# Seven block products for the gate and up projections of a dense layer, and another order of the work where the attention begins

## What is computed

```python
Wg = (gate_w.astype(float32) - 128.0) * gate_scale[:, None]   # 2048 x 512, int32 weights
Wu = (up_w.astype(float32) - 128.0) * up_scale[:, None]       # 2048 x 512
Wd = (down_w.astype(float32) - 128.0) * down_scale[:, None]   # 512 x 2048
h = silu(x @ Wg.T) * (x @ Wu.T)
x = layernorm(x + h @ Wd.T)
```

## Time and profile before

| | |
|---|---|
| median of 3 runs | 2914.81 us (2914.24 to 2915.42) |
| the profiled execution | 2915.48 us |
| its span, first to last instruction | 2913.7 us |
| TensorE busy | 2875.1 us, 99% of the span |
| VectorE, ScalarE, GpSimd busy | 2190.2, 1463.0 and 1416.7 us |
| mean granted clock of TensorE | 0.997 |
| dense layer, from the gate and up of unit 2 | 384.4 us to 785.1 us |
| slots of the attention | from 785.1 us |

### The profile page before, as it was taken

One profiled execution on the slowest core, in us unless ns is written; L12 is line 12 of the kernel. 1 busy time (PEld: TensorE's weight loads), 2 busy tenths in 40 slices (PEclk: granted clock), 3 DMA queues, 4 the chain that ended last, 5 costly groups with the idle time before them and its releaser, 6 DMA issues.

```text
span 2913.7 us, 39448 instructions
## 1 busy us (share of the span) xinstructions
PE 2875.1 (99%) x13614; PEld 2383.3 (82%) x13614; DVE 2190.2 (75%) x3048; ACT 1463.0 (50%) x3034; POOL 1416.7 (49%) x971
## 2 busy tenths in 40 slices
PE   9999999999999999999999999999999999999998
PEld 8887888888888888888888888768777887888886
DVE  6899433333589999999999999887657677766665
ACT  6655312121466666666666666655544444544443
POOL 7886322222334444444444444557544555655553
PEclk9999999999999999999999999999999999999999
DMA  3000100000132222222222222221111111211111
GB/s 135 1 22 26 64 22 22 22 22 8 47 99 64 72 62 62 72 64 62 69 66 62 65 79 61 77 80 52 51 51 44 58 51 44 73 65 58 51 51 44
DMA packets 78181, 160.40 MB, mean 55 GB/s; under 512 B 11168, under 2 KB 19744, under 8 KB 76960
## 3 DMA queue, kind: packets, MB, share of 16 engines
q1 hardware_dynamic: 77984, 157.88, 17.9%
HBM read 115.63 MB, written 8.65 MB: 43 GB/s over the span
## 4 chain that ended last, share of the span: by engine, by line
PE 92%; DVE 5%; ACT 1%; issue 1%; DMA 0%; POOL 0%; SPq 0%; POOLq 0%; DVEq 0%; ACTq 0%
PE OP L44 8%; PE OP L45 8%; PE OP L46 8%; PE B L44 5%; PE B L46 5%; PE A L44 5%; PE A L46 5%; PE B L45 5%; PE A L45 5%; PE S L1054 3%; PE S L1056 3%; PE S L1055 3%; PE S L1718 2%; PE S L45 2%; PE S L46 2%; PE S L44 2%
## 5 line engine op out<-in xcount | busy, mean ns | idle before, releaser
L1130 DVE SCALAR_TENSOR_TENSOR x_tok<-OP,expert_weight,x_tok 128x512 f32<-128x512 f32 x252 | 188.3, 748 | 144.8 <-PE OP L46 144.5
L1009 POOL TENSOR_TENSOR middle_w_lo<-second_raw,middle_w_hi 128x512 fp32r<-128x512 f32 (+1 forms) x96 | 144.8, 1510 | 223.2 <-ACT middle_w_hi L1004 223.2
L2465 POOL TENSOR_TENSOR lag_rnorm<-lag_norm,minus_half 128x8 f32<-128x8 f32 x64 | 105.9, 1654 | 302.0 <-DVE lag_norm L2763 302.0
L771 POOL TENSOR_TENSOR ffn_in_lo<-ffn_inner,ffn_in_hi 128x512 fp32r<-128x512 f32 x64 | 85.6, 1338 | 335.9 <-ACT ffn_in_hi L767 335.8
L1102 POOL TENSOR_TENSOR middle_in_lo<-middle_slot,middle_in_hi 128x512 fp32r<-128x512 f32 x128 | 168.0, 1312 | 137.6 <-ACT middle_in_hi L1098 136.6
L44 PE MATMUL B<-xT_hi,lag_w_hi 128*128 128x512 f32 x512 | 206.7, 404 | 1.8 <-DVE lag_c L2528 1.8
L44 PE MATMUL A<-xT_hi,lag_w_hi 128*128 128x512 f32 x512 | 200.9, 392 | 0.0
L46 PE MATMUL B<-xT_hi,lag_w_lo 128*128 128x512 f32 x512 | 200.8, 392 | 0.0
L46 PE MATMUL A<-xT_hi,lag_w_lo 128*128 128x512 f32 x512 | 200.5, 392 | 0.0
L45 PE MATMUL B<-xT_lo,lag_w_hi 128*128 128x512 f32 x512 | 199.5, 390 | 0.0
L45 PE MATMUL A<-xT_lo,lag_w_hi 128*128 128x512 f32 x512 | 199.5, 390 | 0.0
(11 more groups left out here) (550 smaller groups left out, 9020.1 us busy)
## 6 DMA issues: line engine op xcount, KB each, us to landing
lag_raw<-in_head_weights SPq DMA_DIRECT2D x64, 256.0 KB, 4.4
lag_b_row<-lag_b_scratch SPq DMA_DIRECT2D x64, 256.0 KB, 3.2
lag_rot_q<-lag_r SPq DMA_DIRECT2D x128, 128.0 KB, 2.3
lag_rot_k<-lag_r SPq DMA_DIRECT2D x128, 128.0 KB, 2.4
middle_down_raw<-in_expert_down SPq DMA_DIRECT2D x32, 512.0 KB, 3.5
middle_raw<-in_expert_in SPq DMA_DIRECT2D x32, 384.0 KB, 2.9
second_raw<-in_expert_in SPq DMA_DIRECT2D x32, 384.0 KB, 3.0
ffn_raw<-in_dense_gate SPq DMA_DIRECT2D x8, 512.0 KB, 3.5
```

The costliest lines, as they stand in the source:

```text
L1009: pool.tensor_tensor(self.w_lo[q % 2][:, out], self.raw[q % 2][:, of], f32(self.w_hi[q % 2][:, out]), ALU.subtract).then_inc(self.s_wlo, 1)
L1130: dve.scalar_tensor_tensor(row, self.down_bank(v, n), self.expert_weight[:, e:e + 1], row, op0=ALU.mult, op1=ALU.add).then_inc(self.s_acc, 1)
L2465: pool.tensor_tensor(rnorm[f.rbuf], norm2, half[:, 0:2 * TPB], ALU.pow).then_inc(s_rn, 1)
```

## The change

Units 0 and 1 (LEADING = 2, four chunks) stay as they are. The other twelve chunks go through seven block products as in the experts, for two batches at a time: 24 steps q, of which q % 2 is the pair of batches and q // 2 the chunk (`DensePairs`). A step has down products of one chunk, 8 tiles of 3 matmuls, each with an add of its own by VectorE. There is one buffer for the weights and one for their parts; the sums S1 to S3 are written into the place of their own low parts. Since the activations stay the same for all chunks, their four sums for each pair are made once (`DenseRows`), by VectorE, in ten subtractions and additions of 128x1024 for each pair, from the high and low parts, with four high parts by ScalarE and four low parts by VectorE. This lies within the end of unit 0 and unit 1.

TensorE's order at the end: the turn of batch 0 stands between the down tiles of the last step, the turn of batch 1 moves into slot 0 behind the first factor row, the turn of batch 2 behind the second, and batch 3 stays. The norms follow. In unit 0, ScalarE makes the high part of batch 2's second chunk ahead of the norm's rows of batch 3, no longer behind them. The rest of the attention and the experts stay. The diff is cut; the waits of `DenseRows.second`, `third` and `fourth` are of the kind of `first`.

```diff
+    def first(self, dve, p):
+        v = self.value
+        dve.wait_ge(self.turned.s_lo, (2 * p + 2) * TPB)
+        self.step(dve, p, "T1", v("hi", p, "B12"), v("hi", p, "B11"), ALU.subtract)
+        dve.wait_ge(self.s_sum, self.summed(p, 1))
+        self.step(dve, p, "T1", v("lo", p, "T1"), v("lo", p, "B12"), ALU.add)
+        dve.wait_ge(self.s_sum, self.summed(p, 2))
+        self.step(dve, p, "T1", v("lo", p, "T1"), v("lo", p, "B11"), ALU.subtract)
...
+    BLOCK = 2 * P
+    PARTS = {1: ("A11", "B11", 0), 2: ("A12", "B21", 1), 6: ("S2", "T2", 0), 7: ("S3", "T3", 0),
+             5: ("S1", "T1", 2), 4: ("A22", "N4", 0), 3: ("S4", "B22", 2)}
...
+    RAW = ("A21", "A11", "A12", "A22", "S4")
+    GROUPS = ((0, 2), (2, 5), (5, 7))
...
+    def sums(self, dve, w):
+        part, out = self.part, self.summed
+        at = self.mats + 6 * w
+        if w:
+            self.done(dve, 7, 2 * w - 1)
+        else:
+            self.closed(dve)
+        dve.wait_ge(self.s_sum, at + 1)
+        dve.tensor_tensor(out("S1"), part("A21"), part("A22"), ALU.add).then_inc(self.s_sum, 1)
+        dve.tensor_tensor(out("S3"), part("A11"), part("A21"), ALU.subtract).then_inc(self.s_sum, 1)
+        dve.wait_ge(self.s_sum, at + 2)
+        dve.tensor_tensor(out("S2"), out("S1"), part("A11"), ALU.subtract).then_inc(self.s_sum, 1)
+        dve.wait_ge(self.s_sum, at + 4)
+        dve.tensor_tensor(part("S4"), part("A12"), out("S2"), ALU.subtract).then_inc(self.s_sum, 1)
...
+    def split_hi(self, act, w, n):
+        act.wait_ge(self.s_sum, self.mats + 6 * w + (1, 4, 5)[n])
+        if w:
+            self.done(act, (2, 7, 3)[n], 2 * w - 1)
+        else:
+            self.closed(act)
...
+    def split_lo(self, pool, w, n):
+        pool.wait_ge(self.s_whi, self.mats + 4 * w + n + 1)
+        if n == 1:
+            pool.wait_ge(self.s_sum, self.mats + 6 * w + 5)
+        out, of = self.group(n)
+        pool.tensor_tensor(self.w_lo[:, out], of, f32(self.w_hi[:, out]), ALU.subtract).then_inc(self.s_wlo, 1)
...
+        out, first = self.bank(n, q), p in self.OPENS
+        pe.wait_ge(self.s_wlo, self.mats + 4 * (q // 2) + self.NEEDS[p])
+        if q < 2 and x in self.rows.ORDER:
+            pe.wait_ge(self.rows.s_lo, self.rows.place(q, x))
+        if p == 1:
+            pe.wait_ge(self.s_in, self.products + (2 * (q - 2) + 1 if q > 1 else 0))
+        elif p == 2 and q > 1:
+            pe.wait_ge(self.s_c, self.at["c", 11, q - 2])
+        elif p == 5 and q > 1:
+            pe.wait_ge(self.s_c, self.at["c", 12, q - 2])
+        elif p in (2, 5) and q == 1:
+            pe.wait_ge(self.s_acc, self.tiles_before - TPB + n)
+        elif p in (6, 7, 4):
+            pe.wait_ge(self.s_act, self.at["act", {6: "snap1", 7: "snap2", 4: "snap3"}[p], q])
+        elif p == 3:
+            pe.wait_ge(self.s_c, self.at["c", 22, q])
...
+        if self.closes(q):
+            pe.wait_ge(self.s_in, self.products + 2 * self.last)
+            pe.wait_ge(self.s_acc, self.tile(q, n) - 3)
+        else:
+            pe.wait_ge(self.s_acc, self.tile(q, n) - 1)
...
+    def tiles(self, q, p):
+        if q < 1:
+            return ()
+        if q == self.last:
+            return [(q - 1, n) for n in {4: (4, 5), 3: (6, 7)}.get(p, ())]
+        if q == self.last - 1:
+            return ([(q - 1, n) for n in {1: (0, 1), 2: (2, 3), 4: (4, 5), 3: (6, 7)}.get(p, ())]
+                    + [(q, n) for n in {5: (0,), 7: (1, 2, 3)}.get(p, ())])
+        return [(q - 1, n) for n in {1: (0,), 2: (1,), 4: (2,), 3: (3,), 6: (4,), 5: (5,), 7: (6, 7)}[p]]
...
-                sp.wait_ge(dense.s_wlo, (UNITS - 1) * 3)
+                sp.wait_ge(dense.s_deq, LEADING * 3)
+                pairs.load(sp, 0, a["dense_in"])
+                pairs.load_out(sp, 0, a["dense_out"])
+                for w in range(1, DENSE_CHUNKS):
...
+                for q in range(pairs.last):
+                    for p in (1, 2, 4, 3, 6, 5, 7):
+                        pairs.product(pe, p, q if p in (4, 3) else q + 1)
+                        for step, n in pairs.tiles(q, p):
+                            pairs.down(pe, step, n)
+                for p in (4, 3):
+                    pairs.product(pe, p, pairs.last)
+                    for step, n in pairs.tiles(pairs.last, p):
+                        pairs.down(pe, step, n)
+                for first, tiles in ((0, (0,)), (2, (1, 2)), (4, (3,))):
+                    pairs.down(pe, pairs.last, first)
+                    pairs.down(pe, pairs.last, first + 1)
+                    turn1.turn(pe, 0, [A, T, S1, O], norm1.s_row, lambda t: pe.wait_ge(
+                        pairs.s_in, pairs.products + 2 * pairs.total), tiles)
+                pairs.down(pe, pairs.last, 6)
...
-                        pe.wait_ge(turn1.s_lo, max(f.s + 1, 2) * TPB)
+                        pe.wait_ge(turn1.s_lo, (f.s + 1) * TPB)
                     until(pe, s_cv, f.s * TAPS)
                     projection(f, 0, A, s_a1)
                     until(pe, s_sz, f.s - 1)
+                    if f.s == 0:
+                        pairs.added(pe, pairs.last, TPB)
                     if f.s == 1:
                         pe.wait_ge(turn1.s_lo, BATCH * TPB)
                     projection(f, 1, B, s_a2)
                     if f.s == 0:
...
+                        pe.wait_ge(turn1.s_lo, 2 * TPB)
+                        factors.product_row(pe, 1)
+                        turn1.turn(pe, 2, [S0, S1, T, O], norm1.s_row)
                         factors.turn_row(pe, 1)
```

ScalarE in the steps, and its order where slot 0 begins; then VectorE's:

```diff
+                for q in range(pairs.last):
+                    pairs.snap(act, 1, q + 1)
+                    if q % 2:
+                        if q < pairs.last - 1:
+                            pairs.split_hi(act, (q + 1) // 2, 1)
+                    else:
+                        pairs.down_split_hi(act, q // 2)
+                    pairs.silu(act, 0, q + 1)
+                    if q % 2 == 0 and q < pairs.last - 1:
+                        pairs.split_hi(act, (q + 2) // 2, 0)
+                    pairs.high(act, 0, q)
+                    if q == 0:
+                        pairs.snap(act, 2, 1)
+                    pairs.silu(act, 1, q)
+                    if q % 2 and q < pairs.last - 1:
+                        pairs.split_hi(act, (q + 1) // 2, 2)
+                    if q:
+                        pairs.snap(act, 2, q + 1)
+                    pairs.high(act, 1, q)
+                    pairs.snap(act, 3, q + 1)
+                pairs.done(act, 7, pairs.last - 1)
+                split_head(0, 0, range(5))
+                factors.split_hi(act)
+                pairs.high(act, 0, pairs.last)
+                norm1.normalise(act, 0, tiles=(0,))
+                pairs.silu(act, 1, pairs.last)
+                norm1.normalise(act, 0, tiles=(1,))
...
                         norm1.normalise(act, 3, tiles=(0, 1))
-                        factors.row(act, 0)
-                        norm1.normalise(act, 3, tiles=(2, 3))
-                        turn1.high(act, 2)
...
-                        if u == UNITS - 1:
-                            dense.added(dve, u, t)
-                            norm1.statistics(dve, t)
-
+                pairs.dequantise(dve, 0)
+                chunks_of(dense, 1, 1)
+                dense.add(dve, 1, 0)
+                dense_rows.low(dve, 0, "T1")
+                dve.wait_ge(dense.s_u, FPU * (BATCH + 2))
+                dense_rows.fourth(dve, 0)
+                dense_rows.low(dve, 0, "T2")
+                chunks_of(dense, 1, 2)
+                dve.wait_ge(dense.s_wlo, 6)
+                dense_rows.first(dve, 1)
+                dense.add(dve, 1, 1)
+                dense_rows.low(dve, 0, "T3")
+                dense_rows.low(dve, 0, "N4")
+                dense_rows.second(dve, 1)
+                chunks_of(dense, 1, 3)
+                pairs.sums(dve, 0)
+                dense.add(dve, 1, 2)
+                dense_rows.third(dve, 1)
+                dense_rows.low(dve, 1, "T1")
+                pairs.corner(dve, 11, 0)
+                dense_rows.fourth(dve, 1)
+                dense.add(dve, 1, 3)
+                dense_rows.low(dve, 1, "T2")
+                pairs.dequantise_out(dve, 0)
+                dense_rows.low(dve, 1, "T3")
...
+                for q in range(pairs.last):
+                    pairs.corner(dve, 22, q)
+                    if q % 2 == 0:
+                        if q < pairs.last - 1:
+                            pairs.dequantise(dve, (q + 2) // 2)
+                    elif q < pairs.last - 1:
+                        pairs.sums(dve, (q + 1) // 2)
+                    tile_adds(q, 1)
+                    pairs.corner(dve, 11, q + 1)
+                    tile_adds(q, 2)
+                    pairs.inner(dve, 0, q)
+                    tile_adds(q, 4)
+                    pairs.corner(dve, 12, q)
+                    if q == 0:
+                        dense_rows.low(dve, 1, "N4")
+                    tile_adds(q, 3)
```

(51 more changed lines are left out.)

425 lines of the change are left out of this document (340 added, 85 removed).

## The result

The changed kernel takes 2888.80 us in the median of 4 runs (2886.67 to 2889.11), against 2915.11 us (2914.24 to 2916.76) for the kernel before beside it. The ratio is 0.9906, with a 95% interval from 0.9895 to 0.9918: 26.3 us less, where 25.7 were forecast. The profiled execution took 2888.55 us, its span is 2886.8.

The account below looks back on a forecast made before the run. The prediction took TensorE, busy 99% of the span, as the bound: -32.6 + 1.2 + 3.0 + 2.7 = -25.7 us, from 2914.8 to 2889 us. Four cases in five lie between 2882 and 2900.

Parts of the forecast that it names:

- The matmuls: Dense layer: block products remove 144 gate and up matmuls at 0.2267 us each, -32.6 us.
- The steady state: Middle dense steps of 14.96 us: VectorE's 11 to 12.5 us fit and weight swaps have 1.5 to 2.4 slack; nothing lost.
- both rivals that end near or above the time before: Stalls at each of 11 weight swaps, 2922 us, chance 0.05; stalls of about 1 us in all 24 steps, 2913, chance 0.05.
- the second: Stalls of about 1 us in every one of 24 steps from pairs of adds on two banks, 2913 us; chance 0.05.
- Going in: Entry to the new steps: product 3 of step 0 waits for VectorE's corner 22, +1.2 us.
- Ahead of the attention: Last step before the attention: TensorE waits for an add and for the turned rows' low parts, +3.0 us, bounds 0 and 6.
- Slot 0: Attention's first slot: VectorE's statistics delay the taps, and the turn of the squares waits for ScalarE; +2.7 us, bounds 0 and 6.
- No clock lost: Whole kernel: granted clock stays at 1.00, as single waits are 1.4 us at most; nothing added.

Follow-up runs that it names:

- experiment 1: Kernel before, with 144 gate matmuls of units 2 to 7 left out and nothing else changed; 2883.21 us against 2915.81.
- experiment 4: Changed kernel with six extra VectorE operations ahead of the third block sums of the second pair of batches; 2890.46 us.
- experiment 3: Changed kernel with six extra GpSimd operations ahead of its low part of S1 to S3 at each of 11 weight swaps; 2903.18 us.
- experiment 8: Changed kernel with six extra VectorE operations behind corner 22 in each of 23 steps; 2918.85 us, ratio 1.0012.
- 2: Changed kernel with three extra GpSimd operations ahead of its low part of S1 to S3 at each of 11 weight swaps; 2887.63 us.
- 6: Changed kernel with VectorE reordered ahead of the attention: first inner part and an add before batch 0's last two statistics, batch 1's first two later; 2890.70 us.
- 9: Changed kernel with the order ahead of the attention changed on VectorE, GpSimd, ScalarE and TensorE; 2889.89 us.
- 10: Changed kernel with VectorE's statistics of batch 3 behind slot 0's first taps and ScalarE's rows of batch 3 behind both squares; 2887.13 us.
- 12: Changed kernel with three extra VectorE operations behind corner 22 in each of 23 steps; 2889.33 us.
- 5: Changed kernel with VectorE's statistics and aggregates of batch 3 moved from ahead of slot 0's first taps to behind them; 2887.26 us.
- 7: Changed kernel with both VectorE reorderings: ahead of the attention, and batch 3's statistics behind slot 0's first taps; 2891.04 us.

## Why the prediction was right

**The matmuls** (-32.6): right, shown by experiment 1, to 0.1 us in its trace. A step is 14.96 us, there are 13470 matmuls.

**The steady state** (nothing lost): right. VectorE has 10.7 us of 14.96 to do on average, just under the 11 to 12.5 given. The slack at the swap is 2.8 us, more than the 1.5 to 2.4 counted: every sum took its 0.41 us and GpSimd stood still, as had been taken, and ScalarE's high part starts behind S2, the third sum, and not behind the fourth. The mechanisms of both rivals that end near or above the time before exist, and were a measured distance away: 2.8 us at the swap, about 1.8 in an odd step. The prediction gave both 0.05; the second is the nearer.

**Going in** (+1.2): no wait, so this term was wrong in size. VectorE kept to the forecast's times up to the low part of T1 (over at 391.4, as forecast), where block sums below the assumed 1.3 made up for two weight sums of 1.5 us (the 382.22 row is one). What failed lies behind it: `fourth` took 2.4 us in place of 3.6, since no wait for GpSimd came, and two low parts, the dequantising and the corner took 0.5 less than counted, which makes the 1.8 us by which corner 22 was over ahead of 402.0. Product 3, due at 400.9 by the forecast, came at 401.28. The mechanism was right, as experiment 4 shows with the wait at product 3 under a delay of 2.7. The 0.54 us ahead of 384.96 lie within the 1.7 by which that point moves between executions; no cause was sought.

**Ahead of the attention** (+3.0): measured 2.90, with waits of 0.92 and 0.97 us where 1.4 and 1.2 were forecast, and tile (22,3) late by 0.4 where 0.3 was said. The rows' idle leaves out 0.16 us of each wait (0.39 - 0.23, experiment 3), and the matmul behind the one that waited comes at 0.34 us in place of 0.23; that and some tenths around the turns are the rest. Two sizes too high and one cost left out made a sum that fits: in part luck.

**Slot 0** (+2.7): measured 2.3. The wait for the taps is 0.56, not 1.4: VectorE's operations start some 0.08 us ahead of the end of the one before, which was not counted here, so two batches of statistics took 2.9 us each and not 3.03, and the taps began at 9.2 and not 9.7. The one for the squares is 0.40, not 1.4. The largest, 1.15 us at product row 2, was not named: it is the way of batch 2 from the turn through ScalarE and VectorE back to TensorE, with nothing put between. The prediction also read the trace before wrongly: three batches' statistics are over there when slot 0 begins, not two, and the row at 760.70 is batch 1's. The term does not rest on it. The sum came near and its parts did not: that is luck.

**No clock lost**: right for the changed kernel's profiled execution, at 1.00 throughout the dense layer and slot 0, though an idle of the same 1.15 us cost clock in run 4 (below).

## What to carry to other kernels

Where TensorE is busy for 99%, count matmuls: the gain is their number times their spacing, and the seams are a separate sum of a few us. Before taking out a wait at a seam, ask which engine is full up to that point, what stands behind the wait on every queue, and what the operation that is put back leads to; here each wait could be moved and the end came earlier by nothing that the measurement tells apart. A slack is worth measuring with a delay of known length on the engine in question, since nothing shows until it is used up: 1.35 us a step on VectorE were free, 2.7 took the whole gain.

## What was not expected of the hardware

A wait costs more than its row's idle: 1.16 us at a swap cost 1.46, and 0.77 and 1.02 in experiment 8 lengthened two steps by 2.4. Of each, 0.16 is the way the rows count; the other 0.1 to 0.15 is real, as the matmul after the one that waited comes 0.34 us behind it.

The clock does not follow from the length of a wait alone. In slot 0, ahead of product row 2, an idle of 1.15 us left it at 1.00 in the changed kernel and in 2, 3, 6, 8, 9, 10 and 12; in 4 the two stretches of 5 us behind the same idle have 0.84 and 0.82. An idle of 1.81 in 5 left it at 1.00, while in 7, two waits of 0.80 and 1.94 us within 5 us brought it down to the lower level, 1.2 GHz, for a whole stretch:

```profile
775.00:780.00 5.00, 4.84 (x11) 3.80 (x12) 4.47 (x8) 2.18 (x4) 1.28 (x1) 0.50 0.79 243
```

Matmuls of 128x512 stand 0.43 us apart there in place of 0.2267. In 7 slot 0 takes 30.9 us, in 4 28.6, against 27.5: the clock makes reorderings at a seam worth 1 us a gamble of the same size. The four executions of 10 show a spread of that size, and order themselves by the mean granted clock: 2885.61 us at 0.997, 2889.29 at 0.995. What decides it is open.
